# Two-layer decoder: the passes over the next maxima move to another place in the order of layer 0's and layer 1's attention loops

## The reference, cut to what matters

```
# layer 0
sim = jnp.einsum('bihd,bjhd->bhij', q, k) * SCALE
attn = jax.nn.softmax(sim, axis=-1)
out = jnp.einsum('bhij,bjhd->bihd', attn, v)
# layer 1, for (Wa, ba) in (att0, att1)
kv = bitnet_linear(image_embeds, Wa, ba)
k = jnp.concatenate([kv, kv], axis=-1)
scores = jnp.einsum('bse,bpe->bsp', fused, k) * inv_sqrt_e
attn = jax.nn.softmax(scores, axis=-1)
fused = fused + 0.1 * jnp.einsum('bsp,bpe->bse', attn, k)
```

## Time and profile before

| | |
|---|---|
| median of 3 runs | 1639.53 us |
| profiled execution, its own time | 1638.51 us |
| its span, first to last instruction | 1636.8 us |
| mean granted TensorE clock | 0.964 of full speed |
| PE busy, DVE busy, ACT busy, POOL busy | 93%, 79%, 69%, 30% of the span |
| instructions | 27033 |

### The profile page before, as it was taken

How to read it: one execution, slowest core, us unless ns; L and a number is a source line. 1 busy time by engine, 2 the same in 40 slices (tenths; PEclk the granted TensorE clock), 3 DMA queues, 4 the chain that set the end, 5 groups by cost and what they waited for, 6 DMA issues and landing times.

```text
span 1636.8 us, 27033 instructions
## 1 busy us (share of the span) xinstructions
PE 1530.1 (93%) x9058; PEld 548.9 (34%) x9058; DVE 1286.3 (79%) x2319; ACT 1126.0 (69%) x1541; POOL 490.9 (30%) x488
## 2 busy tenths in 40 slices
PE   6889999999999999999999998899997979999986
PEld 4312333333333333333333223344444612222223
DVE  6898987879977779878789897877775666787766
ACT  6787777768877778777777786655554469676643
POOL 6303343334543334433300010345451012233100
PEclk9759999999999999999999998999999979999998
DMA  4000000000200000000010000111100000000000
GB/s 135 7 1 11 1 1 1 1 2 11 54 1 2 1 1 1 3 1 11 20 32 3 1 1 19 37 46 45 45 27 1 1 1 2 0 1 1 1 14 13
DMA packets 14834, 22.79 MB, mean 14 GB/s; under 512 B 1990, under 2 KB 11766, under 8 KB 14710
## 3 DMA queue, kind: packets, MB, share of 16 engines
q1 hardware_dynamic: 14710, 21.22, 4.6%
HBM read 20.69 MB, written 0.52 MB: 13 GB/s over the span
## 4 chain that ended last, share of the span: by engine, by line
PE 69%; issue 11%; DVE 9%; POOL 5%; ACT 4%; DMA 0%; POOLq 0%; SPq 0%; DVEq 0%; ACTq 0%
PE PS L2167 22%; PE PS L2153 15%; PE PS L2511 6%; PE PS L2199 5%; POOL WRK L734 5%; PE PS L2498 3%; DVE KNB L1382 3%; PE PS L2020 2%; PE PS L2012 2%; PE PS L2116 2%; PE PS L2540 2%; PE PS L2450 1%; PE PS L2435 1%; PE PS L2004 1%; ACT KNB L959 1%
## 5 line engine op out<-in xcount | busy, mean ns | idle before, releaser
L1382 DVE CUSTOM_DVE_ANT_0 KNB<-PS,KNB 128x512 f16<-128x512 f32 (+2 forms) x500 | 338.5, 690 | 152.4 <-PE PS L2199 106.9
L1432 DVE TENSOR_TENSOR WRK<-WRK 128x768 f32<-128x768 f32 (+3 forms) x400 | 425.2, 1063 | 15.3 <-ACT WRK L933 8.4
L933 ACT ACTIVATE WRK<-PS 128x1024 f32<-128x1024 f32 (+1 forms) x408 | 401.4, 1022 | 47.6 <-PE PS L2153 39.2
L2167 PE MATMUL PS<-WRK,V 128*64 128x512 f32 (+1 forms) x1632 | 395.7, 605 | 0.0
L708 POOL TENSOR_TENSOR WRK<-WRK 128x256 f32<-128x256 f32 x300 | 274.7, 916 | 395.6 <-ACT WRK L933 394.6
L959 ACT ACTIVATE KNB<-PS 128x512 f16<-128x512 f32 (+2 forms) x306 | 180.9, 591 | 77.8 <-PE PS L2199 77.2
L2344 PE MATMUL PS<-WRK,KNB 128*128 128x512 f16 x828 | 188.3, 381 | 7.1 <-POOL WRK L734 2.7
L2167 PEld LDWEIGHTS PS<-WRK,V 128*64 128x64 f32 (+1 forms) x1632 | 99.3, 136 | 192.7 <-issue 154.5
L2153 PE MATMUL PS<-KNB,KB 64*128 64x512 f16 (+1 forms) x1224 | 156.5, 377 | 0.0
L2153 PE MATMUL PS<-Q,KB 64*128 64x512 f16 (+1 forms) x1224 | 153.0, 377 | 0.0
L1162 ACT ACTIVATE WRK<-PS 128x1024 f32<-128x1024 f32 x100 | 102.4, 1024 | 51.1 <-PE PS L2498 47.6
(11 more groups left out here) (379 smaller groups left out, 1834.2 us busy)
## 6 DMA issues: line engine op xcount, KB each, us to landing
V<-in_moe_w_dram SPq DMA_DIRECT2D x44, 192.0 KB, 2.4
KNB<-in_ctx_fm_dram SPq DMA_DIRECT2D x6, 384.0 KB, 8.4
X<-in_ctx_fm_dram SPq DMA_DIRECT2D x12, 192.0 KB, 2.4
CTX<-in_ctx_fm_dram SPq DMA_DIRECT2D x6, 384.0 KB, 3.9
BW<-in_bit_w_dram SPq DMA_DIRECT2D x1, 960.0 KB, 9.8
PWK<-in_pair_w_dram SPq DMA_DIRECT2D x4, 192.0 KB, 2.8
XT<-in_x_fm_dram SPq DMA_DIRECT2D x1, 512.0 KB, 5.0
X<-in_x_tm_dram SPq DMA_DIRECT2D x1, 512.0 KB, 12.0
```

Source lines behind the costliest of these rows:

```text
L933: e.activation(PR[0:r, u % 2, b, :], bank(2 * b, 2 * b + 2, slice(0, r)), ACT.Exp).then_inc(S("exp"), 1)
L1382: return e.tensor_tensor_reduce(diffs, sums, diffs, 0.5, NEG, ALU.add, ALU.max, accum_out=out)
L1432: e.tensor_tensor(total, total, part, ALU.add).then_inc(S("acc"), 1)
L2167: ins = e.matmul(PS[h * HD:(h + 1) * HD, 4, :], V[0:r, j, h * HD:(h + 1) * HD], PR[0:r, unit_no(hf, i) % 2, b, h * HALF:(h + 1) * HALF], s ...
```

## The change

The number of instructions stays as it is but for layer 1's split value products. Layer 0: `mid` moves from between the two score products to behind both, on PE and on ACT; `last` stays in its place where a slot makes values for the next pair. Layer 1: a unit with one step (quarters 1 and 2) takes it behind the scores instead of ahead; a unit with two steps takes its second between two halves of `values1` (256 of 512 columns each) instead of right behind the scores. ACT's and DVE's orders follow.

```diff
+def before_scores(n, i):
+    return steps1(n, i)[0:1] if len(steps1(n, i)) > 1 or n == 0 else []
...
@@ ACT, layer 0
                     exp(hf, i, 0)
-                    magnitude(p, mid)
                     for x in filter(inside, ITEMS[p][s]):
                         bank5(x)
                     if len(tiles_of(i)) > 1:
                         exp(hf, i, 1)
+                    magnitude(p, mid)
                     magnitude(p, last)
...
@@ ACT, layer 1 (DVE's maximum1 and add_up1 alike)
-                    magnitude1(n, steps1(n, i)[0:1])
+                    first = before_scores(n, i)
+                    magnitude1(n, first)
                     exp1(n, i)
-                    magnitude1(n, steps1(n, i)[1:])
+                    magnitude1(n, steps1(n, i)[len(first):])
...
@@ PE, layer 0
                     scores(hf, i, 0)
-                    max_steps(p, mid)
...
                         scores(hf, i, 1)
+                    max_steps(p, mid)
+                    makes_values = any(x[0] == "v" for x in ITEMS[p][s])
                     for x in ITEMS[p][s]:
                         if x[0] == "v" and mid:
                             bank5(x)
-                    max_steps(p, last)
+                    if makes_values or not mid:
+                        max_steps(p, last)
...
                             values(*before, b)
+                            if b == 0 and mid and not makes_values:
+                                max_steps(p, last)
...
@@ PE, layer 1
+                parts = (0, HALF // 2, HALF) if steps else (0, HALF)
+                for a, b in zip(parts, parts[1:]):
+                    if a:
+                        max_steps1(quarter, steps)
+                    for g in tiles_of(i):
+                        ins = e.matmul(PS[g * HD:(g + 1) * HD, 4, a:b], V2[n // 2][0:w, j, :],
...
-                    max_steps1(n + 1, steps1(n, i)[0:1])
+                    first, second = before_scores(n, i), steps1(n, i)[1:]
+                    max_steps1(n + 1, first)
                     scores1(n, i)
-                    max_steps1(n + 1, steps1(n, i)[1:])
+                    if not first:
+                        max_steps1(n + 1, steps1(n, i)[0:1])
+                    if i < 2:
+                        max_steps1(n + 1, second)
                     for x in ITEMS1[n][i]:
                         bank5_1(x)
-                    if i:
+                    if i >= 2:
+                        values1(n, i - 1, n + 1, second)
+                    elif i:
                         values1(n, i - 1)
```

More of the change, by code:

```diff
@@ L1900, in _ @@
                 for i in range(NU):
-                    maximum1(quarter, steps1(quarter, i)[0:1])
+                    first = before_scores(quarter, i)
+                    maximum1(quarter, first)
                     if i:
@@ L1905, in _ @@
                         add_up1(quarter - 1, NU - 1)
-                    maximum1(quarter, steps1(quarter, i)[1:])
+                    maximum1(quarter, steps1(quarter, i)[len(first):])
                     for x in ITEMS1[quarter][i]:
@@ L2500, in scores1, with values1 @@
                 ins.then_inc(S("sc"), 1)
-            def values1(n, i):
+            def values1(n, i, quarter=0, steps=()):
                 t = turn(n, i)
@@ L2507, in values1 @@
                     e.wait_ge(S("o_ev"), 2 * PAIRS + n)
[L2508 to L2513, removed]
+                parts = (0, HALF // 2, HALF) if steps else (0, HALF)
[3 more added lines that the diff above has]
+                    for g in tiles_of(i):
+                        j = 2 * i + g
+                        w = rows_of(j)
+                        ins = e.matmul(PS[g * HD:(g + 1) * HD, 4, a:b], V2[n // 2][0:w, j, :],
+                                       PR1[t % len(PR1)][0:w, g * HALF + a:g * HALF + b], start=(i == 0),
+                                       stop=(j >= KT - 2), skip_group_check=True)
                 ins.then_inc(S("pv"), 1)
```

## The result

The changed kernel takes 1649.62 us (median of 6 runs, 1648.45 to 1650.81) against 1639.47 for the kernel before (median of 6 runs, 1639.24 to 1643.72). The medians are 10.15 us apart, which is 1.0062; the ratio over all runs is 1.0058, 95% interval 1.0045 to 1.0071. The change makes the kernel slower. The forecast was 1650.0, slower. The profiled execution of the changed kernel took 1649.84, its span is 1648.1.

What follows compares the result with a forecast made beforehand. PE, busy 93% of the span, was taken to set the end. Terms of 7.1 + 2.4 + 0.5 + 0.6 = 10.6 us on the median 1639.53 gave 1650.1, rounded to 1650.0, with a range of 1641.5 to 1656.

Steps and rivals of the forecast that it cites:

- Layer 0, middle step: Layer 0 slots with three steps: PE's 0.43 stall goes, but the last step waits for ACT's Abs; 12 slots 0.57 longer.
- Layer 0, the late slots and slot 48: Layer 0: three slots like 44, where DVE is late already, 0.09 longer each; slot 48 counted among those 0.57 longer.
- Layer 1, a single step behind the scores: Quarters 1 and 2: next first step 2.47 after the scores' start, a 0.49 wait; six units +2.94, the seventh 2.46 to 2.47.
- Layer 1, the second step in halves: Layer 1 two-step units: a half takes 0.58; unit 2.78 to 2.46 ahead of a single-step unit, 2.85 ahead of another two-step.
- The rival with halves as dear as wholes: Layer 1 value products: 256 columns cost 1.01, like a whole, adding +12.0 + 2.6 + 1.3 for 1666; chance 0.08.
- Layer 1, the totals: Layer 1: +2.4 for quarters 1 and 2, +0.5 for quarter 1's key products, +0.6 for quarter 0.
- the seven with key products: Quarter 1 units with a bank-5 key product: later Abs delays ACT's copy; 24.2 against 23.3, 0.5 not yet in the sum.
- the three units: Quarter 0's units with two steps: from 3.13 to 3.35 from one first step to the next, +0.6 for three.
- The last unit of a run: Layer 1: counted as unchanged when totalling the two-step units whose value product is split.
- The sum: Whole kernel: 7.1 + 2.4 + 0.5 + 0.6 = 10.6 slower, a median of 1650.1, rounded to 1650.0.
- the stalls go and nothing replaces them: Rival for both layers: ACT's Abs is never the one waited for, so -15, 1624.6, faster; chance 0.06.
- layer 1's losses don't arise: Rival: layer 0's 7.1 comes, but single steps' Abs get ahead in time; quarters -4.4, total +2.7, 1642.2; chance 0.13.

Runs made afterwards that it cites:

- The experiment with the Abs between the Exps: Changed kernel, but in layer 0 ACT takes the middle step's Abs between the two Exps again, PE's order staying changed: 1639.31 us, ratio 1.0001.
- the experiment with nothing between: Kernel before, with quarter 3's value products cut into two halves of 256 columns that follow each other directly: 1639.70 us, ratio 1.0002.
- Layer 0 alone: Kernel before with only the change's layer 0 part, the middle step behind both scores on PE and its Abs behind both Exps: 1646.01 us.
- layer 1 alone: Changed kernel with layer 0 put back as before, so only the change's layer 1 part remains: 1642.34 us, ratio 1.0017.
- the single Abs first: Changed kernel, but in layer 1 ACT takes a single step's Abs ahead of the unit's Exp: 1644.56 us, ratio 1.0031.
- the single steps alone: Kernel before with only layer 1's single steps moved behind the scores, Abs behind the Exp, value products whole: 1642.21 us, ratio 1.0012.

## Why the prediction was right, and where it was off

**Layer 0, middle step: right in place and size.** The stall of 0.43 went, ACT's Abs became what is late, 0.05 earlier than walked (304.70, 305.41 against 304.75, 305.45), and the slot went from 5.24 to 5.80. In total 6.9 against 7.1. The experiment with the Abs between the Exps shows the cause: one line on ACT takes back 3.4 in each half pair. The lag, the Exp's 0.92 and the readiness of the scores had all been taken from rows, and the walk needed nothing else. One step of it was off without effect: the middle step takes 0.33 ahead of the projection (303.31 to 303.64) and not 0.22, so the last step's stall is 0.99 and not 1.1, but ACT sets when it ends.

**Layer 0, the late slots and slot 48.** The prediction had the late slots 0.09 longer; slot 44 goes from 5.73 to 5.80, and its last step waits 0.66 for ACT. Slot 48, with its narrower steps, was counted like slot 40 and is 0.52 longer. With three slots at 0.57 that makes the +2.30 of a half.

**Layer 1, a single step behind the scores: right.** The next first step came 2.43 to 2.44 after the start of the single unit's scores, where 2.47 stood in the prediction, and ACT released it. The missing 0.03 makes 0.2 a quarter.

**Layer 1, the second step in halves: right.** A half measured 0.58, as taken; the unit ahead of a single one 2.46; ahead of another with two steps 2.83 to 2.86 against 2.85. The rival with halves as dear as wholes fell with it, and the experiment with nothing between shows that the number of matmuls is not what costs.

**Layer 1, the totals: too high.** Predicted were 2.4 + 0.5 + 0.6 = 3.5, measured 1.9 in the quarters. Units 7 to 14 of quarter 1 (the seven with key products and the single one in front) came as walked, 24.27 for 24.2 (23.31 before). But of the 0.9 between 24.2 and 23.3 the prediction's own terms for these units make 0.6, so 0.3 was left to add and not 0.5. Three pieces explain most of the rest. In quarter 0 the first of the three units takes 3.35 as predicted and the second is 0.2 longer too, but the third has no step behind it and gains 0.35: +0.1 instead of +0.6. The last unit of a run, counted as unchanged, goes from 2.34 to 2.25. And quarter 2 of the kernel before holds one unit that is 0.38 longer, where a DVE sum took 1.33; the changed kernel doesn't, so 0.48 hides some 0.85. With 0.03 for each single, this makes 0.5 + 0.2 + 0.4 + 0.4 = 1.5 of the 1.6, and with the 0.2 added too much about all of it.

Here is the first of quarter 0's units in the changed kernel, to be compared with the earlier trace rows:

```profile
1365.90 0.39 PE L2558 MATMUL PS<-CTX,Q 64*128 64x512 f16 x2
...
1369.25 0.39 PE L2558 MATMUL PS<-CTX,Q 64*128 64x512 f16 x2 [0.33 <-DVE MXP L1389]
```

**The sum.** The forecast of +10.6 for a median met +10.15. That it is so close is luck: in the profiled executions the changed stages gave +8.8 of 11.3, and the rest came from stretches that the change doesn't touch and the prediction has no term for. Layer 0 alone and layer 1 alone are +6.8 and +3.1, together 9.9. So the parts add up as medians too, within their intervals; but 1.2 of layer 1's 3.1 is not in its quarters. The direction and the place of the loss were not luck: layer 0's part was walked right to 0.2.

**The rivals.** That the stalls go and nothing replaces them was wrong. With both Abs left early on ACT, PE's new order does make the kernel faster, but by 4.3 (1635.02) and not by 15 (1624.6), since DVE's maximum is late next. That layer 1's losses don't arise was wrong at each step that it names.

## What to carry to other kernels

A step that is handed from one engine to a second and back is only as early as its place in the second engine's in-order queue: moved on PE and on ACT alike it made the kernel 10 us slower, moved on PE with its Abs left early on ACT 4.3 us faster. So walk the queue of every engine in the chain with the times of the trace, and ask after each wait taken away which one ends last then; here it was DVE's maximum in both loops. Decide for each unit by what follows it: with the single steps behind the scores, the same split takes a unit from 2.78 to 2.46 ahead of a unit with one step, and gains nothing ahead of one with two (2.83 to 2.98).

## What the runs showed of the hardware that was not expected

The stretch from the MoE to the first seed of layer 1 has the same instructions in all versions. It took 102.1 to 102.5 in eight traces, 105.1 to 105.2 in three (the changed kernel, the single Abs first, the halves with nothing between) and 103.6 in one more. That this is a difference between executions and not of the code is shown by the version with nothing between its halves: up to quarter 3 its program is the kernel before, and it took 105.2 where that took 102.1. The windows of the traces (stretch: length; busy us and instructions of PE, PEld, DVE, ACT, POOL; granted clock; DMA share, GB/s) differ in the clock. Of the kernel before:

```profile
1239.00:1254.00 15.00, 13.03 (x95) 7.42 (x93) 11.69 (x34) 6.15 (x10) 0.00 (x0) 1.00 0.00 0
...
1299.00:1314.00 15.00, 12.95 (x63) 6.15 (x62) 13.39 (x54) 1.83 (x12) 0.38 (x1) 1.00 0.00 0
```

Of the changed kernel, each 6 us later, by which the work had moved:

```profile
1245.00:1260.00 15.00, 13.28 (x76) 7.31 (x75) 10.08 (x33) 5.43 (x9) 0.00 (x0) 0.89 0.00 0
...
1305.00:1320.00 15.00, 13.74 (x71) 7.83 (x71) 13.06 (x54) 3.50 (x14) 0.38 (x1) 0.89 0.00 0
```

The granted clock was 0.89 in these windows in place of 1.00: for a part of them it lay at the lower of its two levels (1.2 and 2.4 GHz). PE isn't busy throughout in them, 13.0 to 13.7 of 15 us in both kernels. Over the whole stretch the mean granted clock is 0.90 in the kernel before, 0.89 in the trace at 103.6 and 0.87 in the three traces at 105.1 to 105.2; DVE and ACT are busy equally long in all of them. Why one execution is granted less than another is open. For a change worth 10 us, 3 us in one profiled execution is the size of a term: stages must be compared, not spans.

The differences in quarter 0 go with the clock as well, which is still at the lower level at the first seed: over the first 4.7 us its mean is 0.66 in the kernel before, 0.63 in the version with nothing between its halves and 0.61 with the single steps alone, and the same code takes 67.44, 67.56 and 67.62.

The tail from the first seed of quarter 3 is 100.4 in the kernel before and 101.0 to 102.6 in the six versions that have the halves in every unit with two steps, and 100.0 to 100.5 in the five others. No instruction there was changed but for the version that cuts quarter 3's products. Quarter 3's last value product starts 50.5 us behind its first seed in all (its second half 0.3 later where it is cut); what differs lies in the 50 us behind that, and there too it goes with the clock. The mean granted clock of these 50 us is 0.88 to 0.89 in the kernel before and the five others, and 0.86, 0.86, 0.83, 0.83, 0.82 and 0.81 in the six, whose tails are 0.6, 0.6, 0.7, 0.7, 1.2 and 2.2 longer than before. DVE and ACT are busy equally long there; only PE's busy time grows. Why the clock is granted less in just these six is open.
